# GpSimd's side work behind the result transfers of a mixture-of-experts kernel: keys' low parts in half as many pieces, and where two small copies stand

## The reference

```python
xn = _layernorm(x, axis=-1)
# attention, per sequence; key width 64
scores = (xn @ w_q) @ (xn @ w_k).T * 64 ** -0.5, causal
att = softmax(scores) @ ((xn @ w_v1) @ w_v2)
# 16 experts, each token goes to its best one only; F = 256
logits = xn @ w_router.T
mask = one_hot(argmax(logits)); s = sigmoid(logits) * mask
gate, up = split((s * xn) @ gate_up_proj[e])          # 128 -> 2 x 256
expert_out = (up * silu(gate)) @ down_proj[e]         # 256 -> 128
shared = silu(xn @ w_gate.T) * (xn @ w_up.T) @ w_down.T
out = x + att + shared + expert_out
```

## Time and profile before

| | |
|---|---|
| time, median of 3 runs | 235.84 us (235.73 to 238.3) |
| profiled execution | 234.89 us, of which span of the core 233.2 us |
| PE busy | 212.0 us (91% of the span) |
| POOL busy | 158.1 us (68%) |
| DVE busy | 146.2 us (63%) |
| ACT busy | 128.6 us (55%) |

### The profile page before, as it was taken

One profiled execution on the slowest core, in us unless ns is written; L12 is line 12 of the kernel. 1 busy time (PEld: TensorE's weight loads), 2 busy tenths in 40 slices (PEclk: granted clock), 3 DMA queues, 4 the chain that ended last, 5 costly groups with the idle time before them and its releaser, 6 DMA issues.

```text
span 233.2 us, 5014 instructions
## 1 busy us (share of the span) xinstructions
PE 212.0 (91%) x1415; PEld 182.3 (78%) x1417; DVE 146.2 (63%) x352; ACT 128.6 (55%) x305; POOL 158.1 (68%) x308
## 2 busy tenths in 40 slices
PE   4999999999997699899989999799989998899994
PEld 4978888897785598698767887677767786788794
DVE  3889679788764579879846657365456545304512
ACT  2377777877374556666764543344334424645741
POOL 3475956900788888888111989788988989845910
PEclk9999999999999999999999999999999999999999
DMA  6999999970181117215521122222231220009931
GB/s 132 337 381 300 274 208 200 155 291 3 40 210 45 35 49 179 82 37 135 133 67 42 56 80 54 80 70 65 79 87 52 77 78 10 0 6 285 297 90 46
DMA packets 30021, 28.27 MB, mean 121 GB/s; under 512 B 2579, under 2 KB 27162, under 8 KB 29360
## 3 DMA queue, kind: packets, MB, share of 16 engines
q1 hardware_dynamic: 27472, 23.77, 40.6%
q0 software_dynamic: 2528, 4.24, 5.9%
HBM read 14.28 MB, written 10.50 MB: 106 GB/s over the span
## 4 chain that ended last, share of the span: by engine, by line
PE 57%; POOL 21%; issue 8%; DMA 6%; DVE 3%; ACT 1%; SPq 1%; POOLq 0%; ACTq 0%
POOL scratch L457 14%; PE big L1103 7%; PE acc L1365 7%; PE big L1104 6%; PE big L1105 6%; POOL wel L431 5%; DMA xe<-scratch 5%; PE acc L1283 4%; PE acc L1163 4%; PE mid L1354 3%; PE mid L1264 3%; PE mid L1230 3%; PE mid L1113 2%; PE big L1283 2%; PE mid L1133 2%
## 5 line engine op out<-in xcount | busy, mean ns | idle before, releaser
L505 POOL DMA_INDIRECT y_rows<-y,ids x47 | 47.0, 1000 | 13.1 <-issue 8.2
L457 POOL DMA_INDIRECT scratch<-rows,slot x32 | 33.7, 1054 | 17.8 <-DVE slot L729 12.7
L1283 PE MATMUL acc<-vr_all,pt 128*128 128x128 f32 x246 | 35.9, 280 | 2.8 <-ACT pt L1016 2.1
L859 DVE COPY eht<-mid 128x512 f32<-128x512 f32 (+1 forms) x24 | 16.3, 681 | 33.5 <-PE mid L1354 22.9
L1283 PEld LDWEIGHTS acc<-vr_all,pt 128*128 128x128 f32 x246 | 31.6, 191 | 4.9 <-ACT pt L1016 2.3
L779 DVE TENSOR_REDUCE negmax<-big 128x1 f32<-128x128 f32 (+7 forms) x32 | 23.9, 754 | 18.1 <-PE big L1251 17.5
L1075 ACT COPY y<-acc 128x256 f32<-128x256 f32 (+1 forms) x24 | 8.8, 368 | 43.9 <-PE acc L1365 39.0
L1016 ACT COPY pt<-mid 128x512 f32<-128x512 f32 (+3 forms) x48 | 22.8, 475 | 17.0 <-PE mid L1264 14.9
L1004 ACT ACTIVATE prob<-big,negmax 128x128 f32<-128x128 f32 (+7 forms) x32 | 23.8, 743 | 14.1 <-DVE negmax L779 8.8
L1365 PEld LDWEIGHTS acc<-wed,eht 128*128 128x128 f32 x188 | 24.4, 191 | 3.8 <-issue 2.1
L1365 PE MATMUL acc<-wed,eht 128*128 x188 | 25.1, 276 | 1.3 <-DVE eht L859 1.3
(11 more groups left out here) (141 smaller groups left out, 473.5 us busy)
## 6 DMA issues: line engine op xcount, KB each, us to landing
we_raw<-w_gate_up SPq DMA_DIRECT2D x4, 1024.0 KB, 10.4
scratch<-blank SPq DMA_DIRECT2D x1, 3120.0 KB, 27.8
xe<-scratch SPq DMA_DIRECT2D x24, 130.0 KB
q_raw<-qk_all SPq DMA_DIRECT2D x8, 256.0 KB
k_raw<-qk_all SPq DMA_DIRECT2D x8, 256.0 KB
wed<-w_down SPq DMA_DIRECT2D x1, 2048.0 KB, 32.0
expert_out<-y_rows SPq DMA_DIRECT2D x8, 256.0 KB, 4.7
out<-res SPq DMA_DIRECT2D x7, 256.0 KB, 3.7
```

The source lines that it names most:

```text
L457: pool.indirect_dma_start(scratch, bass.IndirectOffsetOnAxis(ap=slot[:, t:t + 1], axis=0), rows[:, t, :], None).then_inc(row_sent[t % FLY] ...
L505: pool.indirect_dma_start(y_rows, bass.IndirectOffsetOnAxis(ap=ids[:, t:t + 1], axis=0), y[p % NY][:, t % 2, :], None, bounds_check=NT * P ...
L1283: last = pe.matmul(weighed(b, g, r), pt[n % 2][:, cols], v, start=kb == 0 and (r == 0 or own_bank), stop=True, skip_group_check=True)
```

## The change

It touches POOL's side work between the result transfers and nothing else.

- The low parts are made 48 columns at a time, once per pair, ahead of the even transfer 2p (p of 2 and more). There were 43 such operations, now there are 22.
- The high parts stay in 43 pieces of 24 columns, each ahead of the same transfer as before.
- `keep_ids(p + 4)` moves to stand right behind `keep_scores(p + 4)`, ahead of transfer 2p + 1. It stood ahead of transfer 2p + 2. So both small copies of a pair stand in the same gap.

Ahead of an odd transfer there are then scores, ids and a high piece; ahead of an even one a high piece and a low piece of double width.

```diff
-            def k_piece(n):
-                return slice(n * K_PIECE, min((n + 1) * K_PIECE, S))
-
-            def last_keys_hi(n):
-                pool.tensor_copy(k_hi[:, k_piece(n)], k_raw[:, k_piece(n)]).then_inc(k_hi_pieces, 1)
+            def last_keys_hi(half):
+                cols = slice(half * K_PIECE // 2, min((half + 1) * K_PIECE // 2, S))
+                if cols.start < S:
+                    pool.tensor_copy(k_hi[:, cols], k_raw[:, cols]).then_inc(k_hi_pieces, 1)
 
             def last_keys_lo(n):
-                cols = k_piece(n)
-                pool.wait_ge(k_hi_pieces, n + 1)
+                cols = slice(n * K_PIECE, min((n + 1) * K_PIECE, S))
+                pool.wait_ge(k_hi_pieces, min(2 * n + 2, -(-2 * S // K_PIECE)))
                 last = pool.tensor_tensor(k_lo[:, cols], k_raw[:, cols], k_hi[:, cols].bitcast(F32), ALU.subtract)
                 if cols.start < S // 2 <= cols.stop or cols.stop == S:
                     last.then_inc(k_lo_ready, 1)
...
                 for t in range(2 * p, 2 * p + used(p)):
-                    if t and p + AHEAD - 1 + t % 2 < NP:
-                        if t % 2:
+                    if t % 2:
+                        if p + AHEAD < NP:
                             keep_scores(p + AHEAD)
-                        else:
-                            keep_ids(p + AHEAD - 1)
-                    if t and (t - 1) * K_PIECE < S:
-                        last_keys_hi(t - 1)
-                    if t > 1 and (t - 2) * K_PIECE < S:
-                        last_keys_lo(t - 2)
+                            keep_ids(p + AHEAD)
+                        last_keys_hi(2 * p)
+                    elif p:
+                        last_keys_hi(2 * p - 1)
+                        if 1 < p and (p - 2) * K_PIECE < S:
+                            last_keys_lo(p - 2)
                     pool.indirect_dma_start(y_rows, bass.IndirectOffsetOnAxis(ap=ids[:, t:t + 1], axis=0),
...
-K_PIECE = 24
+K_PIECE = 48
```

## The result

| | before | after |
|---|---|---|
| median of the runs | 236.33 us (4 runs, 235.73 to 238.3) | 229.27 us (4 runs, 228.72 to 229.78) |
| profiled execution | 234.89 us, span 233.2 | 229.23 us, span 227.6 |

The ratio is 0.969, 95% interval 0.962 to 0.975: 7.1 us faster by the medians, 5.7 by the profiled executions. The forecast was 3.9, and the range of the prediction ended at 230.3. In later rounds the same two kernels had 236.04 (17 runs, 231.7 to 238.0) and 230.29 (6 runs, 228.0 to 231.0), 5.8 apart. The ratios in this document compare only the quicker runs of each kernel, and the kernel before spreads widely (in the later rounds its quicker runs give 0.988, or 2.9 us, where the medians give 0.976), so I read the experiments by their stage in the trace first, and by ratios and medians second.

What follows compares the result with a forecast made beforehand. POOL, back to back for 98% of the stretch, was taken to pace the expert stage: 2.2 from pairs, 0.4 from the first two, 1.6 of waits, less 0.3, is 3.9; 235.84 - 3.9 = 231.9 us median, range 230.3 to 234.6.

Steps and rivals of the forecast that it cites:

- the ring through the ids: Expert stage: SP's loads wait for POOL's ids, 25.9 us in 9 waits, and PE's transposes wait for the loads.
- 1.6 us of waits: Waits and delays among POOL's first 20 pairs of transfers, 1.6 us above 68.2, counted as gone after the change.
- the last transfer, SP's loads back and PE's work all move by about the same 4 us: End of the kernel: all three shift together by about 4 us, so nothing new is late; priced at nothing.
- PE now keeps a lead: Expert stage: with earlier loads PE gets ahead of POOL, so POOL's 1.6 us of waits are counted as gone.
- Rival D: More than forecast: PE's lead also closes up the drain of the last pairs; 5 us gained, 230.8; chance 0.15.
- POOL's sum: First to 41st transfer: 2.2 from 18 pairs, 0.4 from the first two, 1.6 of waits; 4.2 us earlier.
- my allowance of 0.3: Left out of POOL's 4.2 us for the score copy stretched beside a DVE operation, giving 3.9.
- PE can go towards 2.94 a step: Expert stage: early rows end PE's transpose waits and hide register loads, until POOL at 3.29 a pair paces both.
- A: PE is the bound: two steps stay at 6.76 us, only load waits go; 2.0 us gained, 233.8 median; chance 0.22.
- B: Nothing moves: gap work was covered and the load's landing decides; within 0.7 us, 235.8; chance 0.11.
- C: Slower: POOL's 48-column low piece takes more than twice a 24-column one; 3.2 us slower, 239.0; chance 0.05.
- Priced at nothing: Low parts' readiness: the last is made ahead of transfer 46, by 203.5, before PE's fifth block of scores at 207.7.

Runs made afterwards that it cites:

- e1: Against before: only keep_ids moved to the odd gap, low parts still in 43 pieces of 24 columns; 232.04 us, ratio to before 0.982.
- e7: Against after: high parts also in pieces of 48 columns, one ahead of each odd transfer, four operations per pair; 227.24 us, ratio to before 0.974.
- e2: Against after: keep_ids put back in the even gap, so only the low pieces differ from before; 233.40 us, ratio to before 0.994.
- e8: Against e4: keys still on DVE, keep_ids put back in the even gap; 234.01 us, ratio to before 1.001.
- e4: Against after: POOL makes no key pieces, DVE splits the last sequence's keys in two halves; 226.56 us, ratio to before 0.964.
- e6: No edit against e4, run again beside after on the same chip; 225.79 us, ratio to before 0.965.
- e5: No edit, the kernel after once more; 230.29 us, ratio to before 0.988.

## Why the prediction was wrong, point by point

- **What bounds the kernel.** Right that POOL paces the transfers: with the waits gone and its work unchanged they took 68.38 us (e1; 68.2 by POOL's work alone), and e7 shows POOL as the bound once more in after. What the text did not say is how little room there was beside it: POOL's own work takes 3.41 a pair, and the ring through the ids 3.39 to 3.42 (e2, e8). Shorter gaps alone would soon have run into that ring, as e2 did. The text had the ring, with the chain that shows it, but entered it only as 1.6 us of waits that would go; these did go (1.46 in e1).
- **The step that failed** is "the last transfer, SP's loads back and PE's work all move by about the same 4 us", on which the forecast of 3.9 rests. Once the loads start one gap earlier, PE runs ahead of POOL until the loads hold it again, and it enters the last stage with that lead: 0.9 us in after, 1.4 in e1, against none in e2, which has the pieces alone (5.15 behind the 41st transfer, as before). From that `down` to the end of DVE's last operation it is 27.5 us in nine of the ten profiles, so the lead is kept to the end. The text itself had written that "PE now keeps a lead", and still let PE's work move by no more than the last transfer. Rival D named the lead, with 0.15 of the chance, but priced PE's side of it at three times 0.13, and its 5 us in all fell short of the 5.7 too.
- **POOL's sum** was right in kind and 0.4 us short: 4.62 measured in the row of transfers, 4.2 forecast, or 3.9 with my allowance of 0.3. These 0.7 us and the lead of 0.9 make up nearly all of the 1.8 by which the profiled execution missed (5.7 against 3.9). The pair came out at 3.24, not 3.29, since a high piece that ends a gap takes 0.37 to the transfer and not the 0.40 of a low piece; against that, DVE's two-input operations cost 0.7 us and not 0.3 (last section).
- **The part that was moved** starts the loads earlier, as said, and PE's waits for rows fell from 2.4 us to 0.2. That "PE can go towards 2.94 a step" held only for the first pairs; after that POOL holds it back through the loads, and gaps of 0.4 stay (3.5 us). e4 shows them go when POOL is quicker.
- **From profile to median.** The forecast carried the 0.95 us by which the runs of before lay above the profiled one over to after. After's profiled execution, 229.23, is at its median. That is 0.9 us of the miss in the median, and it says nothing about the change.
- **Rivals.** A (PE is the bound) and B (nothing moves) fell with e7 and with the trace. C (slower) fell with 286 ns.
- **Priced at nothing, rightly:** the low parts. The last one starts at 201.47 in after, PE's fifth block of scores at 205.98.

The version to keep is e4: keys on DVE in two halves, ids in the odd gap. In its second set of runs (e6) it was 4.5 us under after and 10.2 under before by medians of the same rounds; its ratio to before, 0.965, is worth 8.2 (5.7 to 10.8).

## What to carry to other kernels

When two rings have nearly the same pace, what undoing one is worth depends on the other. With the wider low pieces, the two parts gave 2.9 and 2.2 us alone and 5.5 together; with the keys off POOL, that part gave 1.5 alone and 8.9 together with the ids. Before pricing a move by the engine that it stands on, follow what its semaphore starts, and ask who gains a lead from it. A tiny operation that lets a load start belongs in the earliest gap in which its data are there: here its place was worth 2.9 us in before, 3.3 between e2 and after, and 7 where POOL had time to spare, and its length is 0.2. And the end of this kernel moved with PE, which runs the last stage, so a saving is to be followed to where that engine starts it, not to the last operation of the engine that was changed.

## What the runs showed of the hardware

**A wide DVE operation with two SBUF inputs stretches POOL's work, and DMA issues with it.** DVE's `q_hl` operation reads two operands from SBUF. In e1 it ran from 139.23, and a low piece of 24 columns beside it took 0.70 us in place of 0.23; in after it ran from 140.97, and the indirect transfer's instruction itself took 1.44 us in place of 1.00. Timeline of both engines, e1 and after:

```profile
139.23 0.75 DVE L689 SCALAR_TENSOR_TENSOR q_hl<-q_raw,q_hl 64x512 fp32r<-64x512 f32 x1
...
139.37 0.70 POOL L483 TENSOR_TENSOR k_lo<-k_raw,k_hi 128x24 fp32r<-128x24 f32 x1
```

```profile
140.97 0.69 DVE L690 SCALAR_TENSOR_TENSOR q_hl<-q_raw,q_hl 64x512 fp32r<-64x512 f32 x1
141.10 1.44 POOL L504 DMA_INDIRECT y_rows<-y,ids  x1 [0.17 <-issue]
```

The Trainium skill (SBUF — State Buffer, Who interferes with whom) says that a DVE instruction with two SBUF inputs contends with a GpSimd instruction that reads SBUF; both places agree. It adds, as inferred, that a `tensor_tensor` of this kind takes only the read side of the shared ports and that descriptor generation needs the write side; here the indirect transfer, whose offsets are read from SBUF, was 0.44 us longer, and 0.43 in e5. In e4, e6 and e8 five more transfers took 1.27 to 1.38 us, each beside a DVE operation with two SBUF inputs. No run tells whether the read of the offsets or the making of the descriptors was held up.

**A single load can cost 1.5 us more than its neighbours.** The load of pair 10 landed 3.66 us after its issue in the first profile of before, 4.07 in the second and 3.89 in e1, where others take about 2.2. In after the same load took 2.57. In e8 it was the load of pair 6, with 3.50. These times are read from the chains of waits.

In the slow cases the end of the load moved very little: 6 and 11 GB/s over 1 us in e1 and the first profile of before, next to nothing over the last 2 us in the second. An instruction fetch of some 20 KB fell into the load in all four. In after and in e2 such a fetch came as the load ended or just behind it, and these loads took 2.57 and 2.1 us. That the fetch holds one of the DMA engines is a guess that no run tested. The kernels whose loads start earlier lose less to it: PE waited 1.55 us for this load in before, 0.23 in after, nothing in e4; but 1.8 in e1, whose ids were early as well, so the place of the ids alone is no protection.
